# Sixteen-head attention over channels and a routed FFN: deeper rings for the inputs x and x transposed, loaded behind the read of q, k, v

## The reference

```python
query = layernorm(x) @ Wq.T + bq ; key = ctx @ Wk.T + bk ; value = ctx @ Wv.T + bv
logits = einsum('bsid,bsjd->bsij', query, key) / sqrt(16)
out = einsum('bsij,bsjd->bsid', softmax(logits), value)
x = x + reshape(transpose(out, (0, 2, 1, 3))) @ Wd.T + bd
# FFN: one of 8 experts per token, chosen by argmax of a cosine gate
h = gelu(xn @ W1[e] + b1[e]); x = x + (h @ W2[e] + b2[e]) * score
```

## Time and profile before

| | us |
|---|---|
| median of 3 runs | 375.54 |
| lowest and highest | 375.03, 377.86 |
| the profiled execution | 371.7 |
| its span, first to last instruction | 369.9 |
| TensorE (PE) busy | 334.9 (91%) |
| POOL busy | 284.2 (77%) |
| VectorE (DVE) busy | 258.9 (70%) |
| ScalarE (ACT) busy | 193.5 (52%) |
| HBM traffic | 42.00 MB read, 22.07 MB written |

### The profile page before, as it was taken

How to read it: one execution, slowest core, us unless ns; L and a number is a source line. 1 busy time by engine, 2 the same in 40 slices (tenths; PEclk the granted TensorE clock), 3 DMA queues, 4 the chain that set the end, 5 groups by cost and what they waited for, 6 DMA issues and landing times.

```text
span 369.9 us, 11173 instructions
## 1 busy us (share of the span) xinstructions
PE 334.9 (91%) x3755; PEld 286.7 (78%) x3755; DVE 258.9 (70%) x723; ACT 193.5 (52%) x525; POOL 284.2 (77%) x538
## 2 busy tenths in 40 slices
PE   7898699999999978887769996799999999999994
PEld 6686588888877766665647885779999999999993
DVE  6555778888888867788848656795656565656662
ACT  1002658777777758476775736513443435353531
POOL 3667969989898867877888577564777778888874
PEclk9999899999999999999878999999999999999998
DMA  7699979999899999997799012410222222222210
GB/s 236 214 280 286 258 174 252 254 261 273 257 286 259 234 242 297 305 300 195 202 383 374 32 46 72 119 61 29 71 63 73 71 63 71 66 66 74 62 48 1
DMA packets 55415, 63.87 MB, mean 173 GB/s; under 512 B 36558, under 2 KB 45919, under 8 KB 55360
## 3 DMA queue, kind: packets, MB, share of 16 engines
q1 hardware_dynamic: 50832, 52.77, 49.5%
q0 software_dynamic: 3744, 9.53, 8.7%
q10 hardware_dynamic: 784, 0.87, 0.7%
HBM read 42.00 MB, written 22.07 MB: 173 GB/s over the span
## 4 chain that ended last, share of the span: by engine, by line
PE 57%; POOL 18%; issue 10%; DVE 8%; DMA 3%; ACT 1%; DVEq 1%; SPq 0%; POOLq 0%; ACTq 0%
PE bQ L1138 16%; PE bKV L1108 8%; PE bL L1108 7%; POOL x L394 6%; PE bY L996 4%; PE bKV L940 4%; PE bKV L943 4%; PE bQ L1033 3%; POOL cat L374 3%; PE bO L963 3%; PE bL L952 3%; PE bT L1120 2%; POOL cp L357 2%; DMA r<-in_xc 2%; DMA wA<-in_wkvT 2%
## 5 line engine op out<-in xcount | busy, mean ns | idle before, releaser
L1138 PE MATMUL bQ<-w,wA 128*128 x312 | 74.3, 381 | 3.8 <-DVE r L790 3.4
L1138 PEld LDWEIGHTS bQ<-w,wA 128*128 128x128 f32 x312 | 56.2, 190 | 10.9 <-issue 4.9
L394 POOL TENSOR_TENSOR x<-ql,mask 128x1024 f32<-128x1024 f32 x32 | 60.6, 1894 | 0.5
L424 POOL DMA_INDIRECT out<-r,isc x39 | 40.7, 1045 | 16.7 <-issue 12.5
L836 ACT ACTIVATE pad<-ql 64x512 f32<-64x512 f32 x64 | 40.1, 626 | 23.6 <-DMA ql<-qkv_scr 23.2
L447 POOL DMA_INDIRECT r<-row_scr,ig x39 | 40.6, 1042 | 6.1 <-issue 2.1
L1108 PEld LDWEIGHTS bKV<-wA,r 128*128 128x128 f32 x320 | 38.5, 192 | 4.2 <-issue 2.4
L1108 PE MATMUL bKV<-wA,r 128*128 128x128 f32 x320 | 39.4, 276 | 2.4 <-DVE wA L777 1.8
L903 ACT ACTIVATE wA<-bL,r 128x128 f32<-128x128 f32 x76 | 21.7, 369 | 36.8 <-PE bL L1108 36.8
L903 ACT ACTIVATE wA<-bKV,r 128x128 f32<-128x128 f32 x80 | 22.8, 368 | 33.5 <-PE bKV L1108 33.5
L768 DVE TENSOR_SCALAR r<-w1b 128x1028 f32 x39 | 27.8, 712 | 15.5 <-issue 13.3
(11 more groups left out here) (175 smaller groups left out, 662.5 us busy)
## 6 DMA issues: line engine op xcount, KB each, us to landing
qkv_scr<-qkv SPq DMA_DIRECT2D x16, 768.0 KB, 5.9
ql<-qkv_scr SPq DMA_DIRECT2D x32, 384.0 KB, 5.6
r<-in_xc SPq DMA_DIRECT2D x15, 512.0 KB, 6.5
row_scr<-cat SPq DMA_DIRECT2D x32, 133.5 KB, 6.0
w1b<-in_W1b SPq DMA_DIRECT2D x8, 514.0 KB, 6.2
w<-in_W SPq DMA_DIRECT2D x8, 512.0 KB
xt<-in_x SPq DMA_DIRECT2D x15, 256.0 KB, 6.3
b2b<-in_b SPq DMA_DIRECT2D x4, 256.0 KB
```

The source lines that it names most:

```text
L394: eng.tensor_tensor(quarter(kx[:, z % 2, :]), spread(ql[z // 2 % 2][:, :, z % 2, 0:HD]), mask_k, ALU.mult).then_inc(S["kx"], 1)
L424: eng.indirect_dma_start(out, bass.IndirectOffsetOnAxis(ap=isc[k][:, :], axis=0), yo[k], None, bounds_check=NTOK - 1, oob_is_err=False).th ...
L1138: i_ = eng.matmul(bQ[:, 0:C], hT[b % 2][:, k, :], w2[:, bass.ds(eb * (KH * C) + k * C, C)], start=(k == 0), stop=(k == KH - 1))
```

## The change

The rings get deeper: XC from 4 to 6 tiles, XR from 14 to 16. The loads of xc use three semaphores in turn in place of two. In `sync_attention` the load of xc moves: up to t = 5 it stands behind the write as before (t + 3); from t = 7 on it stands behind the read and behind the load of x, and fetches t + 5; a single load (tiles 10 and 11) at t = 6 fills the gap. The load of x behind the read fetches t + 7 in place of t + 5, from t = 7 on. To make room, the space of `x0` goes from 4096 to 3744 numbers per partition, the small tables `io_r1` and `io_k1` lie in a part of `b2b` that is filled only later, and `r1` has 3072 numbers in place of 2312.

```diff
-XR = 14
-XC = 4
+XR = 16
+XC = 6
...
-        io_r1 = sb("io_r1", [P, P])
-        io_k1 = sb("io_k1", [P, NSP])
...
-        x0 = sb("x0", [P, 2 * NH * P])[:, :]
+        x0 = sb("x0", [P, 3744])[:, :]
...
+        io_r1, io_k1 = b2b[:, 6 * C:6 * C + P], b2b[:, 6 * C + P:6 * C + P + NSP]
...
-        r1 = sb("r1", [P, 2 * W1W + C])[:, :]
+        r1 = sb("r1", [P, XC * 4 * P])[:, :]
...
                 if c >= XC:
                     eng.wait_ge(S["qq"], c - XC + 2)
-                eng.dma_start(xcT[:, c % XC:c % XC + 2, :, :], xc[c // 2]).then_inc(S[f"ld_c{c // 2 % 2}"], 16)
+                eng.dma_start(xcT[:, c % XC:c % XC + 2, :, :], xc[c // 2]).then_inc(S[f"ld_c{c // 2 % 3}"], 16)
...
                     eng.dma_start(qkv_scr[p], qkv[p % 2][:, :, :, :]).then_inc(S[f"st_q{p % 2}"], 16)
-                    sync_xc(eng, t + 3)
+                    if t < 6:
+                        sync_xc(eng, t + 3)
                     if t < 8:
                         sync_x(eng, t + 5)
                 sync_row(eng, t - 10)
...
-                    if t > 8:
-                        sync_x(eng, t + 5)
+                    if t > 6:
+                        sync_x(eng, t + 7)
+                        sync_xc(eng, t + 5)
+                if t == 6:
+                    sync_xc(eng, 10)
...
-                    eng.wait_ge(S[f"ld_c{a // 2 % 2}"], (a // 4 + 1) * 16)
+                    eng.wait_ge(S[f"ld_c{a // 2 % 3}"], (a // 6 + 1) * 16)
```

More of the change, by code:

```diff
@@ L56 @@
 PIECES = (("oh_a", 1), ("rv_a", 5), ("rv_a", 10), ("rv_a", 13), ("texp_a", 1), ("selk_a", 1), ("taken_a", 1))
-SEMS = ("ld_xx ld_cc ld_x0 ld_x1 ld_x2 ld_c0 ld_c1 st_q0 st_q1 ld_q0 ld_q1 st_r0 st_r1 st_r2 st_r3 st_r4 ld_wq ld_wkv ld_wd ld_wo ld_g ld_gr ld_gt ld_b ld_bd "
+SEMS = ("ld_xx ld_cc ld_x0 ld_x1 ld_x2 ld_c0 ld_c1 ld_c2 st_q0 st_q1 ld_q0 ld_q1 st_r0 st_r1 st_r2 st_r3 st_r4 ld_wq ld_wkv ld_wd ld_wo ld_g ld_gr ld_gt ld_b ld_bd "
         "ld_bc ld_w1 ld_w2 ld_b2 filled ident iotas const cp mask4 pad0 nmax gpow ctr0 ctr gmm gate gx gxs "
```

## The result

The changed kernel is slower, and by much more than forecast: median 388.77 us against 375.21 us, ratio 1.0347 with a 95% interval of 1.0292 to 1.0402, that is 11 to 15 us. The medians are over all eight executions of each kernel; the ratio leaves out the three slowest of the changed kernel, so it isn't the quotient of the two. The forecast was 379.0 us with a range up to 385.0.

A forecast was written before the change was run, and what follows sets the result against it. From about 80 us the SyncE queue's loop was taken to set the pace; at 11.2 us per pair the attention half ends 2.2 us later, plus 1.3 for uneven transfers: +3.5, 379.0 us on the median 375.54, range 372.5 to 385.0.

The forecast's parts named there:

- the loop of write, turn-round, read, x, row and next write: SyncE queue, attention half: sets the pace of input loads from about 80 us, 10.4 us per pair before.
- The deciding term: Loop in the SyncE queue: xc leaves the turn-round and costs 1.2 us; 10.6 to 11.6 per pair, 11.2 taken.
- The give-back: What the turn-round, emptied of xc, returns to the loop: 0 to 1.0 us per pair, 0.4 taken.
- The walk to the end of the attention half: Writes stepped at 11.2 us from t = 9: tile 30 and the attention half's end 2.2 us late.
- Behind the attention half TensorE is full, so the delay stays.: After the attention half: the delay carries to the end unchanged, total +3.5 us.
- the extra load at t = 6: xc(10) runs ahead of the write of t = 7, which may land up to 1.2 us later; cost zero, 1.2 at most.
- moved tables: Moved tables, smaller x0 and r1, third load semaphore: no instruction added, cost zero.
- rival A: Loop pays in full, nothing given back: 11.6 us per pair, loss from tile 20 on, 383.5 us; chance 0.24.
- near-empty half microseconds after the landed write: Sign of being right: queue share near 0 for two or three half microseconds after each landed write.
- waits for the read: Sign of being right: waits for the read at ACT L836 and POOL L394 from t = 27 on.
- Rival B: Attention half: 2.7 us more slack carries the loads, POOL's in_xc waits vanish; -3.7 at most, 371.8 us; chance 0.12.
- a loop of 10.6 us and -2: If the page's 2 us fixed cost held, the emptied turn-round would give back 1.0: loop 10.6, sum -2.

The follow-up runs named there:

- e1: Kernel before, with only the xc(t+3) load moved behind the read and x from t = 7; old rings and lookahead: 434.92 us, ratio 1.1596.
- e2: Changed kernel with the load of xc(t+5) put back behind the write, so only depth and lookahead are new: 376.14 us, ratio 1.0018.
- e3: Changed kernel with both loads, xc(t+5) and x(t+7), behind the write and none behind the read: 371.66 us, ratio 0.9898.
- e5: Changed kernel with xc loads from tile 12 on cut to 256 bytes per row, part of the computation left out: 374.87 us beside 373.73 us before.
- e6: Changed kernel with the weight loads of t = 22 to 31 moved into the turn-round behind the write: 383.17 us, ratio 1.0240.
- e4: Changed kernel with six instead of five row buffers (cat), a sixth store semaphore and small tables moved: 389.55 us, ratio 1.0338.
- e7: e3 and e6 together: xc, x and the weight loads of t = 22 to 31 behind the write: 369.25 us, ratio 0.9877.

## Why the prediction was wrong

The direction and the mechanism were right: the loop of write, turn-round, read, x, row and next write sets the pace, xc was free in its turn-round and is paid for behind the read. e1, e2, e3 and e5 show it from four sides. Three sizes were off, all to the same side.

- *The deciding term, "10.4 + 1.2 less something from 0 to 1.0", 0.4 taken.* This is the step that failed. The loop is 12.0 us, outside its ends of 10.6 and 11.6: 1.7 us more per pair and not 0.8. From landing to landing, the mean over the five periods from t = 11 to 21 (rounded):

| | before | changed |
|---|---|---|
| landing of the write to that of the read's second half | 7.1 | 7.0 |
| x and row | 1.3 | 1.2 |
| xc | | 1.6 |
| next write | 1.9 | 2.3 |
| period | 10.3 | 12.0 |

 The give-back is 0.1 us and not 0.4, and e5 says the same. The 6.2 of t = 29 in the earlier trace rows was one step, within the spread of the others (6.1 to 7.8 from t = 11 to 25), and I built a term on it. Behind x, xc lands 1.3 us later in four of the five periods and 2.7 in one (t = 19), so the 1.2 was nearly its usual price and the mean is 1.6; and the write behind it takes 0.3 to 0.4 us more. Why one step in five is so long and the write slower, no run shows. With the write of t = 9 already 0.9 late (59.65 in place of 58.77), the landing of the write of t = 21 came at 131.7 in place of 126.0.
- *The walk to the end of the attention half.* The steps of the walk hold with the right loop. Tile 30 is copied 9.0 us later than before (it was forecast 2.2 late), and the last expansion waits for its read, as foreseen:

```profile
165.41 0.52 POOL L360 COPY cp<-r 128x128 f32<-128x128 f32 x2 [1.77 <-DMA r<-in_xc]
...
189.53 1.89 POOL L397 TENSOR_TENSOR x<-ql,mask 128x1024 f32<-128x1024 f32 x1 [1.66 <-DMA ql<-qkv_scr]
...
202.06 1.89 POOL L397 TENSOR_TENSOR x<-ql,mask 128x1024 f32<-128x1024 f32 x1 [2.20 <-DMA ql<-qkv_scr]
```

 202.06 against 190.22 is 11.8 us.
- *"Behind the attention half TensorE is full, so the delay stays."* It grew, from 11.9 us at the expansion of tile 31 (210.10 against 198.18) to 14.9 at the first product with W2 (220.90 against 205.99). The W2 loads of t = 32 to 35 stand in the list behind the read of t = 31, which SyncE can only issue once the write has landed at 195.25. The last two matrices are issued at 204.87 and 205.34 and land 11.9 and 14.2 us later, so the last at 219.5 (205.34 + 14.2). Two waits come of it:

```profile
213.79 0.60 ACT L896 ACTIVATE r<-r 128x256 f32<-128x256 f32 x1 [2.33 <-DMA r<-row_scr,ig]
214.44 0.44 PE L1123 MATMUL bT<-ident,r 128*128 128x128 f32 x2 [2.21 <-ACT r L896]
220.90 1.99 PE L1141 MATMUL bQ<-w,wA 128*128 x8 [1.56 <-issue]
```

 ScalarE waits 2.3 us for rows that POOL has gathered from HBM, and TensorE waits behind it; before it was 0.16, and TensorE's step comes 13.7 us late (214.44 against 200.75). The gather runs while the W2 loads fill the queue, with a share of 1.04 and 1.03 in the 4 us windows from 208 to 216; that they slow it is likely and not shown by itself. Then TensorE, done at 219.34, waits for the last W2: it stands 1.56 us in place of 0.34, 1.2 more. So three more microseconds from a place that the prediction didn't look at. In e6, with the loads earlier, both waits are gone, and 1.0 is left of the 3.0. The median of the runs moved by 13.6 us, about the whole delay.

Of the smaller steps: the extra load at t = 6 made the write of t = 7 land 1.4 us later (48.50 against 47.11), about its limit of 1.2, and cost TensorE nothing (the loss starts at 91 us); moved tables and deeper rings cost nothing (e2). Of what was to be shown: L290 was to start 11.2 apart; it was 12.0, beyond even rival A's 11.6, and the loss began where A put it, at tiles 18 and 20. The near-empty half microseconds after the landed write and the waits for the read came as told. The waits for row_scr weren't foreseen; e4 shows that they don't matter.

Rival B (more lookahead works) is refuted in this placement. In the other, e2, half of it holds: the inputs are early and TensorE keeps 9.86 us up to some 130 us, but the end of the attention half and the W2 loads take the gain back. The rule of the Trainium skill, "Trainium Kernel Development and Optimization", section "Best Practices", to overlap DMA with compute by double buffers is not enough for a serial queue: the time fell when the turn-round was filled (e3), not when the ring alone grew (e2). The other page that was drawn on, "DMA: Bandwidth & Descriptors" of the Trainium skill, section "Anatomy of one DMA", puts a fixed cost of about 2 us on each DMA, mostly the receipt; the section gives it for transfers that GpSimd issues, and these are SyncE's. The sum drawn from it, a loop of 10.6 us and -2, is refuted: the rows above show 3 us at a share under a tenth, from the write's last packets to the read's first, and nothing of it was given back.

What stays open: the last 3 us of the delay between the two profiles (18.1 in the spans, 14.9 at the first W2 product). The changed kernel's execution has a granted clock of 0.91 from 240 to 260 us and 0.83 from 260 to 280, where before has 1.00:

```profile
240.00:260.00 20.00, 16.60 (x99) 14.48 (x99) 15.57 (x42) 10.26 (x28) 12.90 (x26) 0.91 0.30 91
260.00:280.00 20.00, 20.00 (x118) 18.69 (x118) 11.78 (x34) 5.23 (x16) 10.35 (x20) 0.83 0.15 46
```

But the change doesn't seem to be the cause. e2, e3 and e7 have 0.83 from 240 to 260 too, and from the first W2 product to the end e7, the fastest, takes 167.6 us, the changed kernel 167.1 and before 163.9. The profile of before is of an execution of 371.7 us, 3.5 below the median: so a part of the 3 us lies in which executions were profiled. Why some executions have such stretches and others not, no run shows.

## What to carry to other kernels

In a queue that is served in order and in which one transfer must land before the next may be issued, the round trip between them is free room; put the loads that nobody waits for into it, and count every load outside it at its full price, once per loop. More buffers bridge a loop whose sum is above the pace of the compute engine for a while (e2: up to some 130 us), and don't shorten it. Price such a loop over whole periods: the single gap of 1.2 us was nearly the usual one, and the loop still grew by 1.7. Then follow the delay to whatever stands last in the same list.

## What the runs showed of the hardware

A 512 KB load in 128 rows of 4096 bytes landed 1.2 us behind a write that it followed directly, 1.3 us behind x in four periods of five and 2.7 in the fifth, and lengthened the loop by 1.7 us when it stood in the serial part (12.0 with it, 10.3 with 256 bytes per row in its place). Between a write to HBM and the read that waits for it, the share stayed at 0.09 or less for 3 us (118.0 to 121.0 in the changed kernel). The mean DMA share over a stretch of 24 us or more rose to 1.06 and 1.09 in e7; a share of 0.93 wasn't a full queue, though it looked like one, and the share fell to 0.82 as the kernel got slower.
